# Two cross-attention layers on one core: another order for the first loads, the scores, the context's norm and the A pieces

## The reference, cut to what matters

```python
# layer 0: grouped query attention, 32 heads of 32, 8 key heads, 64 context tokens
q = x @ Wq + bq; k = ctx @ Wk + bk; v = ctx @ Wv + bv      # x: (4, 1024, 1024), ctx: (4, 64, 1024)
attn = softmax(q k^T / sqrt(32) + mask)
x = layernorm(attn v @ Wo + bo + x) * gamma + beta
# layer 1: 16 heads of 64; the context is normed first
a = layernorm(ctx) * ln_gamma + ln_beta
Q = x @ Wq.T; K = a @ Wk.T; V = a @ Wv.T
x = x + tanh(gate) * (softmax(Q K^T / 8, keys masked) V @ Wo.T)
```

## Time and profile before

| What | Value |
|---|---|
| runs | 1802.25 us median of 3 (1800.71 to 1804.18) |
| profiled execution | 1800.33 us |
| its span | 1798.5 us |
| PE busy | 1735.8 us of the span, 97% |
| DVE, POOL, ACT busy | 1103.3, 1098.5, 584.0 us |
| mean granted TensorE clock | 0.992 of full |

### The profile page before, as it was taken

One profiled execution on the slowest core, in us unless ns is written; L12 is line 12 of the kernel. 1 busy time (PEld: TensorE's weight loads), 2 busy tenths in 40 slices (PEclk: granted clock), 3 DMA queues, 4 the chain that ended last, 5 costly groups with the idle time before them and its releaser, 6 DMA issues.

```text
span 1798.5 us, 22557 instructions
## 1 busy us (share of the span) xinstructions
PE 1735.8 (97%) x8577; PEld 1443.9 (80%) x8577; DVE 1103.3 (61%) x1073; ACT 584.0 (32%) x667; POOL 1098.5 (61%) x607
## 2 busy tenths in 40 slices
PE   6999999999999799999999998999999999999998
PEld 5788878788888688888888877788888888888887
DVE  6888888888878444544444555446644664466442
ACT  4444444434444433333333322213311331133110
POOL 3677777777787756565655576536543664466431
PEclk9999999999999999999999999999999999999999
DMA  8433332333225557676777754454844474456332
GB/s 219 113 82 81 95 80 74 86 77 76 72 74 161 164 180 242 206 242 209 241 234 234 264 169 134 154 173 134 247 140 165 140 217 147 164 153 198 117 119 103
DMA packets 272367, 278.02 MB, mean 155 GB/s; under 512 B 63226, under 2 KB 223108, under 8 KB 272260
## 3 DMA queue, kind: packets, MB, share of 16 engines
q1 hardware_dynamic: 270068, 274.48, 49.3%
q10 hardware_dynamic: 2192, 2.10, 0.4%
HBM read 174.77 MB, written 101.71 MB: 154 GB/s over the span
## 4 chain that ended last, share of the span: by engine, by line
PE 64%; DVE 15%; issue 8%; POOL 6%; ACT 5%; DMA 1%; SPq 0%; POOLq 0%; DVEq 0%; ACTq 0%
PE ps L53 20%; PE ps L55 20%; PE ps L54 20%; DVE small L1057 3%; DVE pr L1077 3%; ACT pr L827 3%; DVE pT0r L1090 2%; DVE pT1r L1090 2%; DVE xT1r L988 2%; ACT ot L821 2%; PE ps L687 1%; DVE xT0r L988 1%; PE ps L695 1%; DMA wv0r<-in_L_xattn_Wv_dram 1%; PE ps L662 1%
## 5 line engine op out<-in xcount | busy, mean ns | idle before, releaser
L1363 POOL TENSOR_TENSOR x2Tl<-x2r,x2Th 128x1024 fp32r<-128x1024 f32 x32 | 76.8, 2400 | 291.0 <-ACT x2Th L929 291.0
L1163 DVE STREAM_TRANSPOSE x2r<-xd 128x1024 f32<-128x1024 f32 x32 | 68.7, 2147 | 210.8 <-PE ps L55 210.8
L1299 POOL TENSOR_TENSOR pr<-pr,small 128x1024 f32<-128x1024 f32 x64 | 122.8, 1919 | 99.0 <-DVE small L1083 99.0
L929 ACT CAST x2Th<-x2r 128x1024 fp32r<-128x1024 f32 x32 | 33.7, 1052 | 375.7 <-DVE x2r L1163 375.7
L1294 POOL TENSOR_TENSOR pr<-pr,small 128x1024 f32<-128x1024 f32 x64 | 123.9, 1935 | 25.5 <-DVE small L1061 25.5
L1057 DVE TENSOR_REDUCE small<-pr 128x16 f32<-128x1024 f32 x64 | 78.0, 1219 | 78.7 <-ACT pr L827 78.7
L1314 POOL TENSOR_TENSOR xb<-xb,bo 128x1024 f32<-128x1024 f32 x32 | 78.2, 2443 | 78.4 <-DMA xb<-in_x_dram 78.4
L1133 DVE TENSOR_TENSOR y<-ps,xb 128x512 f32<-128x512 f32 x64 | 44.0, 687 | 116.6 <-PE ps L55 113.5
L1328 POOL TENSOR_TENSOR y<-y,bet 128x1024 f32<-128x1024 f32 x32 | 77.7, 2428 | 52.3 <-DVE y L1102 52.3
L53 PE MATMUL ps<-wo0h,oc1l 128*128 128x512 f32 x256 | 103.4, 404 | 4.3 <-DVE y L1133 4.3
L53 PE MATMUL ps<-wo0h,oc0l 128*128 128x512 f32 x256 | 103.0, 402 | 1.7 <-DVE wo0l L1012 1.7
(11 more groups left out here) (371 smaller groups left out, 5492.8 us busy)
## 6 DMA issues: line engine op xcount, KB each, us to landing
o_scratch<-ot SPq DMA_DIRECT2D x256, 64.0 KB, 1.8
ocr<-o_scratch SPq DMA_DIRECT2D x16, 1024.0 KB, 7.9
xb<-in_x_dram SPq DMA_DIRECT2D x32, 512.0 KB, 6.7
x_scratch<-y SPq DMA_DIRECT2D x32, 512.0 KB, 5.2
a_scratch<-ost SPq DMA_DIRECT2D x64, 256.0 KB, 3.5
b_scratch<-ost SPq DMA_DIRECT2D x64, 256.0 KB, 4.6
xd<-x_scratch SPq DMA_DIRECT2D x128, 128.0 KB, 2.9
raw<-b_scratch SPq DMA_DIRECT2D x64, 256.0 KB, 5.6
```

Source lines behind the costliest of these rows:

```text
L1163: nc.vector.transpose(x2r[:].rearrange("p k (t j) -> p t k j", t=TPB), xd[:].rearrange("p t (i k) -> p t k i", k=KT)).then_inc(x2_turned, 1)
L1299: nc.gpsimd.tensor_tensor(heads(v), heads(v), mx.unsqueeze(2).to_broadcast([P, TPB * GRP, KEYS]), ALU.subtract)\
L1363: nc.gpsimd.tensor_tensor(x2T[1][:], x2r[:], f32(x2T[0][:]), ALU.subtract).then_inc(x2_lo, 1)
```

## The change

The first loads: `wkr` and all four x tiles are issued by SP behind the context, the small biases first on ACT's queue, then, once the context has landed, `wvr` and `bv`. PE turns the context before the biases. In the loop, `load_k(u + 1)` stands ahead of the x loads, and the last quarter of Wq (`load_wq(3)`) comes behind `load_k(2)` instead of before the loop. The scores of u-1 stand behind six query steps of u instead of four. The context's norm is made in slots 8 to 17 in another buffer (`ctxe`), stored to a scratch (`norm`), and loaded into `ctxn` in slot 60. Wo is split one group a slot in slots 57 to 64. The A pieces come one a half tile, from 52 to 59, all their low parts are DVE's, and POOL makes the coefficients first in the odd half tiles above 52. Of B's first low parts DVE has five (1, 2, 3, 5, 7), and it has the last `beta` and the last low part of the probabilities too.

```diff
             load_ctx(ctx, ctx_ld)
-            sp.dma_start(brow[:KT], w["bq0"].rearrange("(g p) -> g p", p=P)).then_inc(b_ld, 16)
-            sp.dma_start(brow[KT:], w["bk0"].rearrange("(h p) -> h p", p=P)).then_inc(b_ld, 16)
-            sp.dma_start(bv_row[:], row(w["bv0"], KV0)).then_inc(b_ld, 16)
-            sp.dma_start(wvr[:], w["Wv0"].rearrange("(k p) n -> p k n", p=P)).then_inc(kv_ld1, 16)
-            load_x(sp, 2)
-            load_x(sp, 3)
+            sp.dma_start(wkr[:], w["Wk0"].rearrange("(k p) n -> p k n", p=P)).then_inc(kv_ld0, 16)
+            for n in range(4):
+                load_x(sp, n)
             load_wq(0)
...
-                if u == KT + 3:
+                if u == KT:
+                    load_ctx(ctxe, n_ld)
                     load_norm()
-                if u == 2 * KT:
+                if u == 2 * KT + 1:
+                    store_norm()
+                if u == 2 * KT + 3:
+                    sp.wait_ge(n_st, 64)
                     load_chunk(0)
...
-                    query(range(0, 4))
+                    query(range(0, 6))
...
-                    query(range(4, KT))
+                    query(range(6, KT))
...
-            act.dma_start(wkr[:], w["Wk0"].rearrange("(k p) n -> p k n", p=P)).then_inc(kv_ld0, 16)
-            load_x(act, 0)
-            load_x(act, 1)
+            act.dma_start(brow[:KT], w["bq0"].rearrange("(g p) -> g p", p=P)).then_inc(b_ld, 16)
+            act.dma_start(brow[KT:], w["bk0"].rearrange("(h p) -> h p", p=P)).then_inc(b_ld, 16)
+            act.wait_ge(ctx_ld, 64)
+            act.dma_start(wvr[:], w["Wv0"].rearrange("(k p) n -> p k n", p=P)).then_inc(kv_ld1, 16)
+            act.dma_start(bv_row[:], row(w["bv0"], KV0)).then_inc(bv_ld, 16)
...
-                if u == UNITS + 1:
+                if u == 2 * KT - 1:
                     norm_rows(0)
                     norm_rows(1)
...
+                if wo_groups(u):
+                    split_wo(u - (UNITS - 7))
+                if u == KT + 4:
+                    norm_stats(0)
+                    norm_stats(1)
+                if u == KT + 5:
+                    norm_stats(2)
+                    norm_stats(3)
...
+                seam = h > LEAD + TAB * KT
+                if half == 1 and n + 1 < NTILE and not seam:
                     residual(n + 1)
...
                 if half == 1:
                     coefficients(n)
+                if seam and half == 1 and n + 1 < NTILE:
+                    residual(n + 1)
                 if later:
-                    chunk_lo(h // 4 + 1, 1)
+                    for i in range(0 if seam else 1, 2):
+                        chunk_lo(h // 4 + 1, i)
```

More of the change, by code:

```diff
@@ L190, in program @@
                                                     sems("w1_ld", 2), sems("ost_st", 6))
-        n_ld, n_stat, n_aggr, n_coef, n_applied, n_turned, n_raw, n_hi, n_lo = (sem(n) for n in (
-            "n_ld n_stat n_aggr n_coef n_applied n_turned n_raw n_hi n_lo").split())
+        n_ld, n_stat, n_aggr, n_coef, n_applied, n_st, n_back, n_turned, n_raw, n_hi, n_lo = (sem(n) for n in (
+            "n_ld n_stat n_aggr n_coef n_applied n_st n_back n_turned n_raw n_hi n_lo").split())
         (c1_ld, set_, gated, a_hi, a_loe, a_loo, b_hi, b_loe, b_loo, a_free, b_free, xd_ld, x2_turned, x2_hi, x2_lo,
@@ L246, in load_wo, with load_ctx, store_norm @@
                              .rearrange("(k p) n -> p k n", p=P)).then_inc(w_ld[c], 16)
-            def load_ctx(dst, done):
+            def load_ctx(dst, done, rows=d["ctx"]):
                 for b in range(BATCH):
-                    sp.dma_start(dst[32 * b:32 * (b + 1)], d["ctx"][KEYS * b:KEYS * (b + 1), :]
+                    sp.dma_start(dst[32 * b:32 * (b + 1)], rows[KEYS * b:KEYS * (b + 1), :]
                                  .rearrange("(r p) d -> p r d", r=2)).then_inc(done, 16)
+            def store_norm():
+                sp.wait_ge(n_applied, 2)
+                for b in range(BATCH):
+                    sp.dma_start(d["norm"][KEYS * b:KEYS * (b + 1), :].rearrange("(r p) d -> p r d", r=2),
+                                 ctxe[32 * b:32 * (b + 1)]).then_inc(n_st, 16)
             def load_mask(t):
@@ L370, in slot @@
                     load_k(u + 1)
+                if u == 1:
+                    load_wq(3)
+                if u < UNITS and (u == 1 or u and u % 2 == 0) and (n := 6 + u // 2) < NTILE:
+                    sp.wait_ge(x_turned, n - 3)
+                    load_x(sp, n)
                 if 3 <= u <= UNITS:
@@ L389, in slot @@
                     load_wo(0)
+                if u == UNITS - 7:
+                    load_wo(1)
+                if u == UNITS - 4:
+                    load_ctx(ctxn, n_back, d["norm"])
                 if u == UNITS - 6:
-                    load_wo(1)
+                    load_wo(2)
                 if u == UNITS - 5:
[L393 to L396, removed]
                     load_wo(3)
@@ L777, in norm_rows @@
                 act.wait_ge(n_coef, 5)
-                nc.scalar.activation(ctxn[:, r], ctxn[:, r], ACT.Identity, scale=crstd[:, r:r + 1], bias=cnb[:, r:r + 1])\
+                nc.scalar.activation(ctxe[:, r], ctxe[:, r], ACT.Identity, scale=crstd[:, r:r + 1], bias=cnb[:, r:r + 1])\
                     .then_inc(n_applied, 1)
@@ L1016, in norm_stats @@
                 dve.wait_ge(n_ld, 32 + 64)
-                nc.vector.bn_stats(cst[:, r, n], ctxn[:, r, HALF * n:HALF * (n + 1)]).then_inc(n_stat, 1)
+                nc.vector.bn_stats(cst[:, r, n], ctxe[:, r, HALF * n:HALF * (n + 1)]).then_inc(n_stat, 1)
+            for i in range(4):
+                split_ctx(ctxT, i, i + 1)
             dve.wait_ge(kv_hi, 1)
             nc.vector.tensor_tensor(wk[1][:], wkr[:], f32(wk[0][:]), ALU.subtract).then_inc(kv_lo, 1)
-            for i in range(4):
-                split_ctx(ctxT, i, i + 1)
             for n in range(4):
@@ L1050, in slot @@
                     split_x(n)
-                for g in wo_groups(u - 1):
-                    if g < 7:
-                        split_wo(g)
                 if 2 <= u < UNITS + 2:
@@ L1203, in prepare @@
                         nc.vector.copy_predicated(bias[:, b], km[:, b], zero[:]).then_inc(set_, 1)
-                for c in a0_low(h):
+                if 0 <= (c := h - (LEAD + TAB * KT + 2)) < KT:
                     low(0, 0, c)
@@ L1223, in vector @@
             gamma(NTILE - 1)
-            for c in range(1, KT, 2):
+            dve.wait_ge(scaled, NTILE)
+            nc.vector.tensor_tensor(y[(NTILE - 1) % 3][:], y[(NTILE - 1) % 3][:], bet0[:], ALU.add).then_inc(normed, 1)
+            for c in B0_DVE:
                 low(1, 0, c)
@@ L1334, in out_slot @@
                     residual(0)
-                    norm_coefficients()
-                if half == 1 and n + 1 < NTILE:
+                seam = h > LEAD + TAB * KT
+                if half == 1 and n + 1 < NTILE and not seam:
                     residual(n + 1)
@@ L1347, in out_slot @@
                 later = h % 4 == 1 and 1 < h // 4 + 1 < NCHUNK
-                if later:
+                if later and not seam:
                     chunk_lo(h // 4 + 1, 0)
@@ L1399, in gpsimd @@
             scale(1)
-            beta(NTILE - 1)
-            for c in (2, 4, 6):
+            for c in B0_POOL[1:]:
                 low(1, 0, c)
```

70 lines of the change are left out of this document (31 added, 39 removed).

## The result

| | before | changed |
|---|---|---|
| median | 1801.93 us (20 runs) | 1799.26 us (20 runs) |
| range of runs | 1798.96 to 1806.05 | 1795.76 to 1802.58 |
| profiled execution, span | 1800.33, 1798.5 us | 1797.70, 1795.9 us |
| ratio, 95% interval | | 0.9983, 0.9976 to 0.9990 |

A forecast was written before the change was run, and what follows sets the result against it. PE bounds the kernel between stalls, except in the attention, where a chain of waits without PE does. Terms of 0.9, 9.7, 6.0, 5.5 and 1.2 us sum to 23.3, off the median of 1802.25: 1779 us, range 1768 to 1789.

The forecast's parts named there:

- start of the attention's chain: First query 4.7 us earlier, less 1.4 for two later query steps, plus 0.5 at the third scores.
- norm in the chain: Attention slots 12 to 16: statistics cost 0.6 us, aggregates and coefficients 0.7, rows 2.4; together 3.7 lost.
- a pair of slots, lead at slot 56, Wo in slot 57: Attention: a pair stays 17.1 us, PE's lead at slot 56 gains 1.1, splitting Wo in slot 57 costs 0.3.
- seam: After the attention: waits for ctxn and low parts go, full clock returns; 9.7 us gained (7 to 11).
- middle: Earlier coefficients remove the wait for y, 4.3 us, and 2.7 of half clock, less 1.0: 6.0 gained (1 to 7).
- first output: Layer 1's first output: 12.1 us of waits and half clock fall to 6.6; 5.5 gained (3 to 9).
- tail: Kernel's end: the last low part moves from POOL (2.4 us) to DVE (1.21), under a 1.6 wait; 1.2 gained.
- the start is bound by bytes: Rival at the start: only load order changes, first query stays at 34.6 us, forecast loses 4.7, giving 1784; chance 0.12.
- 1.4 for the two steps: Attention's start: two more query steps, 6 matmuls of 0.227 us, delay the first scores by 1.4 us.
- the slower rival: Attention: scores two steps later lengthen the chain, up to 38 us over 27 pairs, 1817 us; chance 0.06.
- a second sum: Middle: DVE and POOL contending cost two odd half tiles up to 1.1 us each, giving 1781 instead of 1779.
- 1.0 for half clock: Layer 1's first output: 1.0 us charged for half clock, where 3.7 had been placed before the change.

The follow-up runs named there:

- a_wv_first: The changed kernel with Wv loaded by SP right behind Wk instead of by ACT's queue: 1793.27 us, ratio 0.9957 to the kernel before.
- a_scores4: The changed kernel with the scores back behind four query steps instead of six: 1797.57 us, ratio 0.9973 to the kernel before.
- b_scores6: The kernel before with only the scores moved behind six query steps instead of four: 1805.32 us, ratio 1.0011 to the kernel before.
- a_norm_idle: The changed kernel with all parts of the norm moved into engines' idle time: 1793.10 us, ratio 0.9946 to the kernel before.
- a_rows: The changed kernel with the two norm_rows moved from slot 15's end to behind slot 16's exponential: 1795.99 us, ratio 0.9963 to the kernel before.
- a_beta_pool: The changed kernel with the last beta back on POOL, ahead of B4's low part: 1798.72 us, ratio 0.9985 to the kernel before.
- c_store: Changed kernel, Wv behind Wk, norm in idle time, scores after four steps, POOL's old order before half tile 57, last y's store ahead of xt loads: 1782.64 us.
- c_store7: c_store with the last y's store also ahead of B7's load: 1782.75 us, ratio 0.9889 to the kernel before.

## Why the prediction was wrong

| Term | forecast, us gained | measured |
|---|---|---|
| start of the attention's chain | +3.8 (4.7 - 1.4 + 0.5) | -3.1 |
| norm in the chain | -3.7 | -6.2 |
| a pair of slots, lead at slot 56, Wo in slot 57 | +0.8 | -1.0 |
| seam | +9.7 | +9.0 |
| middle | +6.0 | +1.6 |
| first output | +5.5 | +1.9 |
| tail | +1.2 | +0.4 |
| sum | +23.3 | +2.6 |

**The start (6.9 of the missing 20.7).** The step that failed is "POOL is earlier too, for `wv` lands earlier; I count that wait as gone". The diff moved Wv behind a wait on ACT, and it landed 1 us later; behind it stood 1.9 + 4.6 us of splitting and the meeting of DVE and POOL, which the forecast priced nowhere. That put the first query 4.8 us behind the forecast. The rival "the start is bound by bytes" gave the right first query (34.6, measured 34.7) for a reason that a_wv_first shows to be wrong. Its reading of the context was loose too: 3.2 and 9.0 us are the quickest and the slowest of the four loads, all beside ACT's queue; with the change the four took 3.1 to 5.0. Half clock cost another 1.6 us between the first query and the first scores: the matmuls ran at 1.2 GHz for 3.4 us, after PE had stood still for 14 of the first 18 us and twice more since; "1.4 for the two steps" held no term for it. But this term is the execution's and isn't shown to be the change's: a_scores4, with the same loads and waits of the same kind, was granted 1.00 at its queries and had its first scores at 43.08, and b_scores6, with the loads of before, was granted 0.51 for 3.3 us at the same place. The last 0.5, for the third scores, did not come: the lag stayed at 3.1 from the first scores to slot 12.

**The norm (2.5).** The mechanism was right, the sizes of two terms were not. The rows were forecast at 2.4 and measured at 2.3. The statistics, "so 0.6", cost 2.0: they pushed the x tile's low part beside POOL's low part of pT, where it took 2.92 us instead of 1.36. Aggregates and coefficients, together "0.7", cost 0.2 and 1.65; the first of POOL's tiny instructions took 1.07 us beside DVE, 0.24 in a_norm_idle.

**The pair of slots (1.8).** That a pair takes 17.11 us "whatever PE does" was nearly right and gave the right picture: PE kept waiting, and the slower rival did not come. But PE's place did matter a little: 0.06 us a pair over 20 pairs is 1.2 us, and the lead at slot 56 with Wo in slot 57 came to 0.2 us instead of 0.8.

**The seam** was right (9.0 of 9.7), and by its steps: no wait for `ctxn`, clock 1.00, 1.0 us left for pT.

**The middle (4.4).** "What is late next is the chunk's low part ... ending about 1 us before or after PE needs them" named the right wait and mis-sized it: two waits, 1.2 and 2.4 us, where 1.0 was charged. That is 2.6 of the 4.4. Most of the rest is the clock, of which 2.7 us were counted as won: the 3.1 us at 1.2 GHz behind the second wait cost 1.4 us where they had cost 2.5 before (against the 11.0 us to the first logits at full clock in a_rows). The residual was moved behind the coefficients in every odd half tile above 52, and in half tile 53 its load had already landed.

The two chunk parts of 2.4 us became 6.7 together. The Trainium skill, page "SBUF — State Buffer", section "Who interferes with whom", says that a VectorE instruction with two SBUF inputs contends with a GpSimd instruction that reads SBUF, and that one with at most one such input, outside the two-port modes, does not. The trace agrees: gamma and the parts of A, with two inputs, took up to 3.4 us beside POOL and 1.2 alone; the statistics, with one, took 1.27 for two everywhere. The forecast cited the section for two half tiles and left its price to a second sum; it should have applied it to the start, to slot 12 and to beta ahead of B1 too.

**The first output (3.6).** The waits from B1 to `x2Tl` were forecast at 5.6 us and measured at 6.5, nearly right in sum and wrong in kind. "B2 and B3 are DVE's now and in time" failed: beta took DVE 3.3 us beside POOL ahead of them, and PE stood 1.6 us for B1 and 1.5 for B3. "B5's cast at 1124" failed too: it came at 1126.9, since the store's landing goes by the queue ahead of it. The larger miss is "1.0 for half clock", with 3.7 before. From the logits of tile 0 to those of tile 4 the kernels took 90.0 and 88.1 us, with 9.2 and 7.4 us of waits (two of 0.4 for `x2Tl` counted in); what is left is 80.8 in both, so the clock gave nothing back there.

The small terms of one execution should not be leaned on. The code of this stretch is the same in eight of the other kernels (all but b_scores6, a_beta_pool, c_store and c_store7). With the changed kernel they took 88.1 to 90.3 us for it, the changed kernel the least, against 90.0 before and 89.8 in b_scores6. So the first output gained 1.9 us at best and perhaps nothing. **The tail (0.8)** gained 0.4 of 1.2: the wait of 1.6 for `probT1l` is gone, and one of 1.2 for DVE's `xt` stands in its place.

The Trainium skill, page "DMA: Bandwidth & Descriptors", section "Queues, rings and completion order", has each DMA engine consume a queue's descriptors in order, though a later one may finish its write first. c_store7 agrees with the order: 8.4 us from issue to cast fell to 5.8 by the store's place in the queue alone.

The common fault: each term was worked out as its own wait, at the durations of before, and what the moved instruction then met on the other engine or in the queue was priced only in the ranges.

## What to carry to other kernels

Where a chain of engines binds, an added instruction costs nothing, or its length, or more than that, by its place: the same 13 instructions of the norm cost 6.2 us at one set of places and 0.1 at another a slot away, found by reading which engine idles, behind what, and for how long. Ask of a moved load or store not only when it is issued but what lies ahead of it in its queue, and of a moved vector instruction which one of GpSimd's it will now run beside. Together, these edits bring the kernel to 1782.7 us, 1.0 to 1.1% below before, most of the way to the forecast of 1779.

## What the hardware showed beyond that

DVE's 128x1024 operations on two tiles took 1.2 us alone and up to 3.42 beside POOL; POOL's 2.40 alone and up to 3.4 beside DVE; POOL's 128x1 additions 0.19 alone and 1.17 beside DVE. And DVE's turn of an x tile took 2.14 us with the scores behind six steps and 2.06 with four, with no other operand or neighbour on DVE changed; its cause is open.

Where half clock falls differs between executions. Seven of the profiled kernels share the changed kernel's first loads. In two of them (the changed kernel and a_rows) 3.3 to 3.4 us at 1.2 GHz fell on the first queries, and the first scores started at 45.9; in three with the same six steps (a_norm_idle, a_pool_order, a_beta_pool) they fell on the values' projection before, and the first scores started at 44.6 to 45.0. A difference of 1 us between two single profiles can be that alone.
